# Selective scan, one core: the decays move to SBUF in a ring of four, the products to PSUM, and three small VectorE tasks go to ScalarE and GpSimd

## The reference, cut to what matters

```
u      = x @ w[cond]                                   # per sequence
dr,B,C = split(u @ x_proj_w.T, (128, 16, 16))
delta  = softplus(dr @ dt_proj_w.T + dt_proj_b)        # [token, 512]
decay  = exp(delta[..., None] * A)                     # 16 states per channel, A < 0
dBu    = (delta * u)[..., None] * B
h[t]   = decay[t] * h[t-1] + dBu[t]                    # h = 0 at a sequence's start
x1     = sum_n h[..., n] * C[n] + u * D  (+ residual x)
q,k,v  = x1 @ Wq.T, x1 @ Wk.T, x1 @ Wv.T               # then rms norm, rotary tables
```

## Time and profile before

| | |
|---|---|
| median of 3 runs | 2159.59 us (2158.35 to 2160.52) |
| the profiled execution's own time, and its span | 2162.24 us, 2160.4 us |
| busy share of the span: TensorE, VectorE, ScalarE, GpSimd | 90%, 72%, 56%, 55% |
| mean granted TensorE clock | 0.966 |

### The profile page before, as it was taken

How to read it: one execution, slowest core, us unless ns; L and a number is a source line. 1 busy time by engine, 2 the same in 40 slices (tenths; PEclk the granted TensorE clock), 3 DMA queues, 4 the chain that set the end, 5 groups by cost and what they waited for, 6 DMA issues and landing times.

```text
span 2160.4 us, 33041 instructions
## 1 busy us (share of the span) xinstructions
PE 1944.0 (90%) x9664; PEld 1344.5 (62%) x9664; DVE 1547.9 (72%) x2697; ACT 1199.8 (56%) x3210; POOL 1196.5 (55%) x1162
## 2 busy tenths in 40 slices
PE   5789998999899899978569999999999999999999
PEld 4666666676667666655246766757566575665755
DVE  6799999999999999999257654545545454554412
ACT  2666676666666666655246654645546454554512
POOL 1477887788877888777577763443443434340000
PEclk8899999999999999999879999999999999999999
DMA  4421332333323332230377443333233323331011
GB/s 141 168 110 66 129 118 90 115 129 129 121 83 121 129 120 107 88 113 30 101 208 246 134 115 96 83 102 104 80 109 93 102 76 96 95 85 37 14 52 47
DMA packets 149546, 225.83 MB, mean 105 GB/s; under 512 B 49859, under 2 KB 109254, under 8 KB 144002
## 3 DMA queue, kind: packets, MB, share of 16 engines
q1 hardware_dynamic: 116306, 161.94, 21.9%
q0 software_dynamic: 31744, 61.07, 10.1%
q10 hardware_dynamic: 1328, 0.91, 0.1%
HBM read 211.44 MB, written 40.51 MB: 117 GB/s over the span
## 4 chain that ended last, share of the span: by engine, by line
PE 43%; issue 2%; POOL 2%; DMA 2%; DVE 1%; ACT 1%; DVEq 0%; POOLq 0%; ACTq 0%
PE attn_psum L1610 11%; PE attn_psum L1624 10%; PE attn_psum L1576 5%; PE attn_psum L1562 4%; PE attn_psum L1549 4%; PE attn_psum L1542 4%; PE attn_psum L1533 2%; PE attn_psum L1640 2%; PE attn_psum L1589 1%; DMA kv<-in_kv_rows,old_now 1%; POOL kv L1214 1%; POOL kv L1206 1%; PE attn_psum L1523 1%; DMA kv<-kv_scratch,new_now 0%; ACT xh L1295 0%
## 5 line engine op out<-in xcount | busy, mean ns | idle before, releaser
L417 POOL TENSOR_TENSOR hid<-hid,bc 128x1024 f32<-128x1024 f32 x256 | 620.6, 2434 | 192.9 <-DVE hid L810 192.3
L938 PE MATMUL scan_psum<-hid,ident 128*128 128x256 f32 x2048 | 540.1, 394 | 108.9 <-POOL hid L417 108.9
L810 DVE TENSOR_TENSOR_SCAN hid<-scan_psum,dbu 128x1024 f32<-128x1024 f32 x256 | 581.7, 2273 | 4.7 <-ACT scan_psum L460 4.6
L938 PEld LDWEIGHTS scan_psum<-hid,ident 128*128 128x128 f32 x2048 | 383.9, 194 | 286.6 <-POOL hid L417 143.8
L460 ACT ACTIVATE scan_psum<-delta,neg_a 128x252 f32<-128x252 f32 x1024 | 423.9, 465 | 122.9 <-DVE hid L810 120.9
L1402 DVE CUSTOM_DVE_ANT_0 prob<-attn_psum,mask 128x336 f32<-128x336 f32 x256 | 120.6, 505 | 384.5 <-PE attn_psum L1542 383.0
L754 DVE TENSOR_TENSOR dbu<-scan_psum,bc 128x1024 f32<-128x1024 f32 x256 | 307.2, 1200 | 0.1
L1263 ACT COPY p_t<-attn_psum 112x384 f32<-112x384 f32 x256 | 121.5, 483 | 293.1 <-PE attn_psum L1549 292.8
L903 PE MATMUL scan_psum<-w_qkv,x 128*128 128x512 f32 x512 | 260.2, 594 | 3.9 <-ACT sq L520 2.4
L1624 PE MATMUL attn_psum<-w,ffn_hid 128*128 128x512 f32 x512 | 239.0, 596 | 8.9 <-DVE y_sb L1454 8.9
L1610 PE MATMUL attn_psum<-xs_in,w 128*128 128x256 f32 x1024 | 238.0, 387 | 0.6 <-ACT th L1296 0.5
(11 more groups left out here) (176 smaller groups left out, 2619.4 us busy)
## 6 DMA issues: line engine op xcount, KB each, us to landing
bc<-bc_scratch SPq DMA_DIRECT2D x32, 2048.0 KB, 7.3
q_scratch<-qg SPq DMA_DIRECT2D x32, 260.0 KB, 2.1
q_in<-q_scratch SPq DMA_DIRECT2D x32, 260.0 KB
x_pair<-in_x_pairs SPq DMA_DIRECT2D x32, 256.0 KB, 2.8
xt<-in_x_tp SPq DMA_DIRECT2D x16, 512.0 KB, 8.4
x_scratch<-x SPq DMA_DIRECT2D x16, 512.0 KB, 2.9
kv_scratch<-kvg SPq DMA_DIRECT2D x32, 256.0 KB, 2.0
w<-in_w SPq DMA_DIRECT2D x8, 1024.0 KB, 9.1
```

What stands on the lines that cost most here:

```text
L417: pool.tensor_tensor(hid[:, r, :, :], hid[:, r, :, :], bc[q // 2][:, 4 * j:4 * j + 4, 1, :], ALU.mult).then_inc(pool_hc, 1)
L810: nc.vector.tensor_tensor_scan(hid[:, k % RING, :, :].rearrange("p n t -> p (n t)"), decay[k % 2], dbu[:, k % RING, :, :].rearrange("p n t ...
L938: mm = nc.tensor.matmul(yc, ident[:], hid[:, k % RING, i, :], start=False, stop=(k % 4 == 3 and i == 3))
```

## The change

Decays go to SBUF in a ring of four, so that the exponentials of a step wait for the scan of four steps back. Products go to PSUM in two buffers, so that `times_b` waits for the scan two steps back; in program order that is the instruction directly ahead of it. `prepare` makes both channel groups of a quarter in one instruction of 512 elements, ahead of the last scan of the quarter before. ScalarE takes the maximum with zero (`Relu`, 512 elements) and the sums of squares (one `Square` with accumulator output for each head: 8 in `take_q`, 4 in `take_kv`). GpSimd takes the addition that makes delta (`step`, behind its product of step 4) and the two key tables (`key_tables`, behind that of step 5).

```diff
-        decay = [psum[:, 2 * i:2 * i + 2, :]... for i in range(2)]
-        du = [psum[:, 4, SUB * i:SUB * i + SUB] for i in range(2)]
+        dbu = [psum[:, 2 * i:2 * i + 2, :]... for i in range(2)]
+        du = psum[:, 4, 0:2 * SUB].rearrange("p (c t) -> p c t", c=2)
-        dbu = sb("dbu", [P, RING, 4, SUB])
+        decay = sb("decay", [P, RING, 4, SUB])
 # gpsimd
+            def step(t, h, q):
+                g = 4 * t + q + 4
+                pool.wait_ge(act_sp, 3 * (g + 1))
+                wait(pool, act_exp, 32 * t)
+                wait(pool, dve_du, 4 * t)
+                pool.tensor_tensor(delta[1 - h][:, :, GRP * q:GRP * q + GRP], zg[:], sp_a[:], ALU.add
+                                   ).then_inc(pool_dl, 1)
+            def key_tables(g):
+                wait(pool, pool_k, 5 * g)
+                for out, table, i in ((k_cos, cos, 0), (k_sin, sin, 1)):
+                    pool.tensor_tensor(... [P, 2, HALF] ...).then_inc(pool_kt, 1)
             def keys(g, p):
+                pool.wait_ge(pool_kt, 2 * (g + 1))
 # behind the product of step k
+                    if k == 4 and parts.second:
+                        step(t, h, q)
+                    if k == 5 and parts.fourth:
...
+                        key_tables(s - 3)
 # scalar
-                    wait(act, dve_h, e - 1)
+                    wait(act, dve_h, e + 1 - RING)
 # add_bias
-                    wait(act, dve_dl, g)
+                    wait(act, pool_dl, g)
 # softplus_exp
+                    nc.scalar.activation(zg[:], zg[:], ACT.Relu)
 # take_q
-                    nc.scalar.activation(sq[:, G:G + H, :]..., pro, ACT.Square).then_inc(act_q, 1)
+                    for i in range(H):
+                        sum_sq = nc.scalar.activation(sq[:, G + i, :], pro[:, HD * i:HD * i + HD], ACT.Square,
+                                                      accum_out=n_ss[:, G + i:G + i + 1])
+                    sum_sq.then_inc(act_q, 1)
 # take_kv: the same with 4 heads; key_rms waits for act_q and act_kv in place of dve_ss
 # vector
                 def times_b
-                wait(dve, dve_h, e + 1 - RING)
+                wait(dve, dve_h, e - 1)
-            def prepare(t, h, b, c): ... 256 elements
+            def prepare(t, h, q):
+                if q % 2 == 0:
+                    dve.wait_ge(pool_dl, 4 * t + q + 2)
+                wait(dve, dve_dbu, 8 * (4 * t + q))
+                ... delta[h][:, c:c + 2, at:at + SUB] x u[h][:, c:c + 2, at:at + SUB] -> du
-                def softplus():
-                def key_squares():
                 for k in range(8):
-                    ... key_squares at k == 3, softplus at k == 4, prepare at k == 2 and k == 6
+                    if k == 7 and parts.next_scan:
+                        prepare(*after)
                     if k < 7 and parts.scan:
                         times_b(t, h, q, k + 1)
-                    if k == 7 and parts.next_scan:
-                        times_b(*after, 0)
                     if parts.scan:
                         ... the scan, with decay[:, k % RING] and dbu[k % 2]
+                    if k == 7 and parts.next_scan:
+                        times_b(*after, 0)
```

More of the change, by code:

```diff
@@ L94, in scan_block @@
         psum = ctx.enter_context(nc.psum_tensor("scan_psum", [P, 8, 512], F32))
-        decay = [psum[:, 2 * i:2 * i + 2, :].rearrange("p b t -> p (b t)") for i in range(2)]
-        du = [psum[:, 4, SUB * i:SUB * i + SUB] for i in range(2)]
+        dbu = [psum[:, 2 * i:2 * i + 2, :].rearrange("p b t -> p (b t)") for i in range(2)]
+        du = psum[:, 4, 0:2 * SUB].rearrange("p (c t) -> p c t", c=2)
         y = [psum[:, 5 + i, :] for i in range(2)]
@@ L150, in scan_block @@
         hid_flat = hid[:].rearrange("p a b c -> p (a b c)")
-        dbu_flat = dbu[:].rearrange("p a b c -> p (a b c)")
-        ang, turns, rem = (dbu_flat[:, 1024 * i:1024 * i + 1024] for i in range(3))
+        decay_flat = decay[:].rearrange("p a b c -> p (a b c)")
+        ang, turns, rem = (decay_flat[:, 1024 * i:1024 * i + 1024] for i in range(3))
         cos = sb("cos", [P, NG * HALF])
@@ L387, in rms @@
                 pool.tensor_tensor(qg[p][:, D:QW], n_r2[:, G:G + H], n_r0[:, G:G + H], ALU.mult).then_inc(pool_qr, 1)
+            def step(t, h, q):
[8 more added lines that the diff above has]
+                for out, table, i in ((k_cos, cos, 0), (k_sin, sin, 1)):
+                    pool.tensor_tensor(
+                        out[:].rearrange("p (a f) -> p a f", a=2),
+                        table[:, bass.ds(g * HALF, HALF)].unsqueeze(1).to_broadcast([P, 2, HALF]),
+                        one_ks[:, i, :].rearrange("p (a f) -> p a f", a=2), ALU.mult).then_inc(pool_kt, 1)
             def keys(g, p):
                 k = 5 * g
+                pool.wait_ge(pool_kt, 2 * (g + 1))
                 pool.wait_ge(pool_rs, g + 1)
@@ L420, in quarter @@
                         weights(s + 6, q % 2)
+                    if k == 4 and parts.second:
+                        step(t, h, q)
+                    if k == 5 and parts.fourth:
+                        if isinstance(t, int) and s == 3:
+                            pool.wait_ge(rope_ok, 1)
+                        key_tables(s - 3)
                     if k == 6 and parts.fourth:
@@ L477, in take_u @@
                     act.wait_ge(pe_u, g + 1)
-                    free = 8 * t + 4 * (q // 3)
-                    wait(act, dve_du, free)
-                    wait(act, pe_res, free)
+                    wait(act, dve_du, 4 * t + 2 * (q // 3))
+                    wait(act, pe_res, 8 * t + 4 * (q // 3))
                     k = (q + 1) % 4
@@ L517, in take_q @@
                     wait(act, st_q[p], 16 * half(t, q - 2))
-                    wait(act, dve_ss, g)
+                    wait(act, act_rs, 3 * g)
                     nc.scalar.copy(qg[p][:, 0:D], pro)
-                    nc.scalar.activation(sq[:, G:G + H, :].rearrange("p h d -> p (h d)"), pro, ACT.Square
-                                         ).then_inc(act_q, 1)
+                    for i in range(H):
+                        sum_sq = nc.scalar.activation(sq[:, G + i, :], pro[:, HD * i:HD * i + HD], ACT.Square,
+                                                      accum_out=n_ss[:, G + i:G + i + 1])
+                    sum_sq.then_inc(act_q, 1)
                 def take_kv():
@@ L529, in take_kv @@
                     nc.scalar.copy(k_raw[:].rearrange("p g d -> p (g d)"), pro[:, 0:G * HD])
-                    nc.scalar.activation(sq[:, 0:G, :].rearrange("p g d -> p (g d)"), pro[:, 0:G * HD], ACT.Square
-                                         ).then_inc(act_kv, 1)
+                    for i in range(G):
+                        sum_sq = nc.scalar.activation(sq[:, i, :], pro[:, HD * i:HD * i + HD], ACT.Square,
+                                                      accum_out=n_ss[:, i:i + 1])
+                    sum_sq.then_inc(act_kv, 1)
                 def key_rms():
                     g = s - 3
-                    act.wait_ge(dve_ss, g + 1)
+                    act.wait_ge(act_q, g + 1)
+                    act.wait_ge(act_kv, g + 1)
                     wait(act, pool_qr, g)
@@ L703, in last_writers @@
                                        ).then_inc(idx_ok, 1)
-                for i in range(2):
-                    ze = v.memset(decay[i].rearrange("p (b t) -> p b t", t=T)[:, :, 0:1], 0.0)
+                for i in range(RING):
+                    ze = v.memset(decay[:, i, :, :].rearrange("p n (b t) -> p (n b) t", t=T)[:, :, 0:1], 0.0)
                 ze.then_inc(zero_ok, 1)
@@ L743, in scales @@
                 dve.wait_ge(c_a, 2)
-                nc.vector.memset(n_ss[:], 0.0).then_inc(rope_ok, 1)
+                dve.sem_inc(rope_ok, 1)
             def times_b(t, h, q, k):
```

27 lines of the change are left out of this document (11 added, 16 removed).

## The result

The changed kernel takes 2260.65 us (median of 6 runs, 2256.53 to 2263.18) against 2160.06 us: 1.046 times the time before, interval 1.045 to 1.047. So it is slower, as forecast, but by 100 us and not by 34.

A forecast was written before the change was run, and what follows sets the result against it. VectorE sets the pace before; afterwards a chain through GpSimd, ScalarE and TensorE makes a quarter 31.4 us. Early quarters +10.0, quarters 4 to 26 +27.8, later ones -9.5, ends and seam: +33.8, so 2193 us; range 2147 to 2226.

The forecast's parts named there:

- the chain: From scan 4 through `step`, `add_bias`, slot 16, `take_q` and the next exponentials: closes in 31.4 us, 1.2 us longer per quarter.
- the squares: ScalarE's `take_q`: 8 squares with accumulator at 0.25 us each, 2.0 us; bounds 0.15 and 0.44 each.
- the prologue: Ahead of the quarters: the `Relu` on ScalarE's chain adds 0.5 us.
- VectorE's 27.7: Scan stage: the time per quarter in us that VectorE alone would need after the change, 2.4 less than now.
- the fourth link: TensorE from slot 16, started at 4.9 us, to the result of `project_qkv(.,0)`: 5.92 us, so done at 10.8.
- Rival 4: TensorE idle ahead of slot 16: clock falls to 1.2 GHz every third quarter, projections up to 11 us; 2230; chance 0.05.
- Rival 1: `take_q` against exponentials 0: exponentials not late for scan 0, quarter 29.7 us, 2151, or about 2100; chance 0.18.
- rival 5: Whole kernel: the change is neutral, a quarter of 30.0 us; chance 0.05.
- Rival 2: ScalarE's `take_q` and `take_kv`: accumulator reads don't overlap, quarter 33.4 us, 2243; chance 0.06.
- Rival 3: Merged `prepare` ahead of scan 7 waits out a GpSimd product, 1.3 us on the mean; quarter 32.7, 2226; chance 0.06.
- The self-wait: VectorE: `times_b` waiting on the scan directly ahead loses the overlap, 0.11 us on each of six steps per quarter.

The follow-up runs named there:

- e1: Changed kernel plus eight matmuls, whose result nobody reads, in TensorE's idle time ahead of slot 16 of quarters 2 to 26; 1.016 times the kernel before.
- e2: Changed kernel with GpSimd's `step` moved from behind product 4 to behind product 3; 0.981 times the kernel before.
- e11: The same kernel as e2 once more, on the third chip and in more rounds; 0.980 times the kernel before.
- e8: Changed kernel with everything put back but the ring, the operands' placement and the merged `prepare`; 0.991 times the kernel before.
- e7: Changed kernel with the softplus maximum and addition back on VectorE ahead of step 4, without `Relu` and GpSimd's `step`; 0.999 times the kernel before.
- e5: The changed kernel once more, unaltered, on the second chip; 1.045 times the kernel before.
- e6: Changed kernel plus three unread matmuls in TensorE's wait ahead of slot 16; 1.030 times the kernel before.
- e3: Changed kernel with ScalarE's single squares back and their sum on VectorE ahead of step 3, `step` still on GpSimd; 1.031 times the kernel before.

## Why the prediction was right and wrong

**The direction was right, and for the reason given.** `add_bias` waits for GpSimd's `step`, the chain closes through slot 16, `take_q` and the next quarter's exponentials, and VectorE, 2.4 us lighter, waits. With the clock held (e1) the quarter is 31.13 to 31.4 us where I had 31.4, and the whole 1.016, or +34 us on 2160 (26 to 42 by its interval), beside the forecast's 33.8. By stretch it is a little less: the last scan ends at 1058.8 us against 1031.9 before, +27, where the terms up to there add up to +31. So the small agreement of the whole owes something to terms that were off in both directions: the squares come every 0.20 us instead of 0.25, and the prologue cost 2.7 instead of 0.5, of which part is scatter (the first scans of the eleven runs lie between 78.0 and 79.8 us). Without the wait (e2, e11) it is 28.0 to 28.3 us beside VectorE's 27.7. e8 puts the ring and the merged `prepare` at 29.45 us, expected at 29.65.

**The step that failed** is the fourth link: "TensorE starts slot 16 at 4.9. From there to the result of `project_qkv(.,0)` it took 5.92 us". The 5.92 came from a row in which TensorE had no idle time ahead of slot 16; I carried it to a place where I had worked out 4 us of idle time myself. It took 8.74, at a granted clock of 0.50, the 1.2 GHz level; with the clock held it takes 5.87 to 6.02 (e1). The 5.92 itself was a sound reading: in the kernel before, the same link takes 5.79 to 6.03 us in every quarter from 2 to 26, always without idle time ahead. (Its rows are of quarter 16, the first behind the loop's seam; only the last one, the scan at 584.80, is quarter 17's.)

**Rival 4 was that very mechanism**, and it was priced too low: at 1.2 GHz in every third quarter, up to 5 us each, with a chance of 0.05. By its rows it is nearly every quarter and 2.7 us on the mean. The mean clock of 0.97, on which I leaned, told of a TensorE that waited 2.8 us at the longest from 200 to 1000 us; it said nothing of one that does in each quarter.

**The other rivals.** Rival 1 (exponentials in time) fell with the late scan 0, and rival 5 (neutral) with it. Rival 2 (accumulator reads that don't overlap) is refuted: the eight activations take 1.6 us. Rival 3 (the lock on `prepare`) didn't come: its mean is 675 ns over 24, forecast 0.66. That the products in PSUM or the decays in SBUF cost more is refuted within 0.03 us: the scan takes 2280 ns (2272 before in the same 800 us), the product 1228 (1200).

**The self-wait** of `times_b` is real: scan start to product start is 2.31 us (869.65 - 867.34) against 2.20, as forecast, and from there to the next scan 1.14 against 1.11. The sentence from the Trainium skill, page "VectorE: DVE Perf Modes", section "The DRAIN you can't avoid", that a semaphore costs nothing would have put the step at 3.31; all runs with the new ring show 3.45. `Relu` takes 613 ns and stands directly between its neighbours, with no table loaded, as the page "ScalarE: Activation LUTs", section "Table sets: the hidden batching unit", of the Trainium skill has it.

## What to carry to other kernels

When a change opens an idle stretch of several microseconds on TensorE inside a loop, price what follows it at both clock levels, in every pass, even if TensorE is far from being the bound; the mean clock of the kernel before says nothing about it. When a task is moved to a later place on another engine, ask who waits in the same pass for its buffer to be read: here one place earlier, or a second buffer of the same data, was worth 6.6% of the whole. And look where an instruction with two SBUF inputs falls against GpSimd's products once the work around it is thinned out: e7 lost there all that it had gained.

## What the hardware showed unexpectedly

In the changed kernel the clock fell behind 3.8 us of idle time in 23 of the 24 quarters from 3 to 26 and not in quarter 3; in e5, the same kernel, in all 24. Behind 2.5 us it fell in 6 of 23 (in e6's quarter 16 the idle time was 0.60 us). What a fall costs varies too: it is 2.8 us of projection in nearly all quarters of the changed kernel, and 1.4 to 1.8 in most of those of e3 and in all six of e6 (8.74, 7.41 and 7.56 against 5.92). ScalarE's activations of 64 elements with accumulator output come every 0.20 us although the activation and the read stand with 248 and 233 ns each, so more than half of a pair's recorded time overlaps that of its neighbours.
